# Three reorderings around an attention loop, and a loop body of two groups instead of one

## What is computed

```python
h = relu(layernorm(x))
q, k, v = h @ Wq.T + bq, h @ Wk.T + bk, h @ Wv.T + bv
scores = where(adj > 0, q @ k.T / sqrt(128), -9e15)
x = x + elu(softmax(scores) @ v)

h = relu(layernorm(x))
g = h @ W
s1, s2 = g @ a[:128, 0], g @ a[128:, 0]
e = where(adj > 0, leaky_relu(s1[:, None] + s2[None, :], 0.01), -9e15)
x = x + g + softmax(e) @ h
```

## Time and profile before

| | us |
|---|---|
| median of 3 runs | 750.28 |
| lowest, highest | 747.99, 750.70 |
| the profiled execution | 749.78 |
| its span, first to last instruction | 748.0 |
| PE busy in it | 716.1 |
| DVE busy | 566.5 |
| ACT busy | 539.8 |
| GpSimd busy | 458.8 |

### The profile page before, as it was taken

The page is one execution under the profiler, slowest core; times in us unless marked ns, Lnnn a source line. Parts: engine busy times, 40 slices in busy tenths (PEclk is TensorE's granted clock), DMA queues, the critical chain, the costliest instruction groups (busy, mean ns, idle before and its releaser), DMA issues. The chain is left out here.

```text
span 748.0 us, 18367 instructions
## 1 busy us (share of the span) xinstructions
PE 716.1 (96%) x6269; PEld 604.4 (81%) x6269; DVE 566.5 (76%) x1201; ACT 539.8 (72%) x1083; POOL 458.8 (61%) x396
## 2 busy tenths in 40 slices
PE   7979999999999999999999999967999999999997
PEld 6657878888888888888888878855888888888886
DVE  6978778787877878788787877759977477577572
ACT  4745877878777687776877778868597797887910
POOL 6778699999999999999999998794000000000000
PEclk9999999999999999999999999987999999999999
DMA  7289999997898988989888873984333442443200
GB/s 239 81 267 258 234 286 235 261 266 232 283 258 245 261 238 281 252 251 261 241 278 245 263 144 81 184 80 85 72 88 75 86 96 64 95 90 68 40 11 13
DMA packets 192783, 132.51 MB, mean 177 GB/s; under 512 B 173536, under 2 KB 180192, under 8 KB 184544
## 3 DMA queue, kind: packets, MB, share of 16 engines
q1 hardware_dynamic: 192000, 131.63, 67.0%
q10 hardware_dynamic: 576, 0.26, 0.1%
q0 software_dynamic: 160, 0.00, 0.0%
HBM read 71.04 MB, written 18.89 MB: 120 GB/s over the span
## 5 line engine op out<-in xcount | busy, mean ns | idle before, releaser
L801 ACT ACTIVATE scores<-scores,neg_max 128x1024 f32<-128x1024 f32 x128 | 146.0, 1142 | 51.8 <-DVE neg_max L932 51.8
L945 DVE TENSOR_TENSOR low<-scores 128x1024 bf16<-128x1024 f32 x96 | 139.7, 1455 | 40.9 <-ACT scores L801 40.9
L1204 PE MATMUL spare<-v_parts,hiT 128*128 128x256 bf16 x768 | 160.5, 273 | 0.0
L363 POOL TENSOR_SCALAR mask_both<-mask_bytes 128x2048 bf16<-128x2048 uint8 x64 | 154.1, 2408 | 5.4 <-POOL mask_bytes L358 0.4
L926 DVE CUSTOM_DVE_ANT_0 scores<-ps_s,mask_both 128x1024 f32<-128x1024 f32 x128 | 155.9, 1218 | 0.4 <-POOL mask_both L363 0.4
L358 POOL TENSOR_SCALAR mask_bytes<-adj_both 128x2048 uint8<-128x2048 int32 x64 | 146.4, 2304 | 5.5 <-DMA adj_both<-in_adj 4.6
L1200 PE MATMUL spare<-v_parts,lowT 128*128 128x128 bf16 x768 | 143.8, 219 | 3.2 <-DMA lowT<-low 3.1
L815 ACT ACTIVATE hiT<-spare 128x512 bf16<-128x512 bf16 (+1 forms) x128 | 102.4, 800 | 36.0 <-PE spare L1174 33.5
L1658 PE MATMUL ps_x<-q_parts,over_k 128*128 128x258 bf16 x1024 | 119.6, 278 | 7.7 <-issue 5.2
L1658 PEld LDWEIGHTS ps_x<-q_parts,over_k 128*128 128x128 fp8e4 x1024 | 100.9, 99 | 25.0 <-issue 5.4
L1139 PE MATMUL ps_s<-k_hi,q_strip 128*128 128x512 f32 x256 | 112.2, 438 | 2.2 <-PEq L83 1.9
(11 more groups left out here) (180 smaller groups left out, 1301.9 us busy)
## 6 DMA issues: line engine op xcount, KB each, us to landing
adj_both<-in_adj SPq DMA_DIRECT2D x64, 1024.0 KB, 5.2
mask_bytes_dram<-mask_bytes SPq DMA_DIRECT2D x32, 512.0 KB, 2.9
x_sb<-in_x SPq DMA_DIRECT2D x8, 256.0 KB, 7.9
out<-res SPq DMA_DIRECT2D x32, 64.0 KB, 1.6
lowT<-low SPq DMA_TRANSPOSE x96, 4.8
mask_both<-s_row_dram SPq DMA_DIRECT2D x2, 768.0 KB, 7.7
over_k<-mask_bytes_dram SPq DMA_TRANSPOSE x16, 4.7
scores<-mask_bytes_dram SPq DMA_TRANSPOSE x16, 4.5
```

What stands on the lines that cost most here:

```text
L363: return nc.gpsimd.tensor_scalar(out, src, -NEG, NEG, ALU.mult, ALU.add)
L801: nc.scalar.activation(sc, sc, ACT.Exp, bias=neg_max[:, bn:bn + 1], accum_out=row_sum[:, bn, k:k + 1]).then_inc(exp_done, 1)
L945: nc.vector.tensor_tensor(low[k][:], p, high_half(p), ALU.subtract).then_inc(low_done, 1)
L1204: last = nc.tensor.matmul(ps_a[:], high, v_parts[:, t, :, :], start=first, stop=final)
```

## The change

Four edits.

1. In the first stage DVE copies the turned weights before it takes the moments of chunk 2, instead of behind them; ACT copies the first `hT` before the third root; PE's wait for the copied weights stands behind its second block of transposes.
2. In period 0 DVE makes both `pT_low` first, then adds masks and takes low parts in turn, with low part 2 last. SP turns low part 0 before it loads strip 3.
3. GpSimd no longer weighs. DVE does `weigh_words(c, 1)` for chunks 0 and 1 behind `weigh(6)`, and GpSimd splits them behind the split of chunk 6.
4. The hardware loop of the attention runs over pairs of groups: three iterations with eight periods each, instead of six with four.

```diff
@@ norm_and_project
             roots(0)
             roots(1)
+            hT_out(0)
             roots(2)
-            hT_out(0)
...
+            hook("vector_early", dve, steps)
             moments_of(2)
             inverse(2)
-            hook("vector_early", dve, steps)
...
                 if c + 1 < NC:
                     to_hT(c + 1)
+                if c == 0:
+                    hook("tensor_first", pe)
...
                     last.then_inc(turn_done, 1)
+
+                def turned_in(pe):
                     pe.wait_ge(turn_read, 3)
@@ all_periods
-                    with eng.Fori(1, NC - 1) as c:
+                    with eng.Fori(0, NC // 2 - 1) as h:
                         for b in range(4):
-                            period(c, b)
+                            period(2 * h + 1, b)
+                        for b in range(4):
+                            period(2 * h + 2, b)
@@ sync
                         if b == 2:
                             store(0, 1)
-                    turn_low(0, 0, 0)
+                            turn_low(0, 0, 0)
@@ gpsimd
-                    def weigh_low(c):
-
-                        pool.wait_ge(s_out, pieces_till(c))
-                        for t in range(4 * c, 4 * c + 4):
-                            last = nc.gpsimd.tensor_scalar(v1[1][:, t, 0:D], h_sb[:, t, :], 0.0, v1[1][:, t, D:D + 1],
-                                                           ALU.max, ALU.mult)
-                        last.then_inc(low_weighed, 1)
-                        pool.wait_ge(low_weighed, c + 1)
-                        split_words(pool, c, 1)
...
                         split_words(pool, c, 0)
-                        if c < LOW_EARLY:
-                            weigh_low(c)
+                        if c == NC - 2:
+                            for n in range(LOW_EARLY):
+                                pool.wait_ge(low_weighed, n + 1)
+                                split_words(pool, n, 1)
@@ vector
                             inverse_sum(s - 1, (b + 3) % 4)
-                        if ahead:
+                        if not has(c, b, -1):
+                            turned_low(s, 0)
+                            turned_low(s, 1)
+                            add_mask(s + 1, bn, 2)
+                            low_part(s, b, 1)
+                            add_mask(s + 1, bn, 3)
+                            find_max(s + 1, bn)
+                            low_part(s, b, 2)
+                        elif ahead:
                             turned_low(s, 0)
                             low_part(s, b, 1)
                             add_mask(s + 1, bn, 2)
...
                     weigh(6)
+                    for c in range(LOW_EARLY):
+                        weigh_words(c, 1).then_inc(low_weighed, 1)
                     add_hw(3)
```

More of the change, by code:

```diff
@@ L518, in build @@
                                       scalar_chunk=first_strips, vector_early=copy_turned, tensor=constants_in,
-                                      tensor_early=turn_weights, tensor_chunk=extras, vector_chunk=copy_extras),
+                                      tensor_early=turn_weights, tensor_first=turned_in, tensor_chunk=extras, vector_chunk=copy_extras),
                                  [(q_product, q_high, q_low), (k_product, k_high, k_low), (v_product, v_high, v_low)],
```

## The result

| | before | changed kernel |
|---|---|---|
| median, us | 750.49 (4 runs, 747.99 to 751.13) | **760.67** (4 runs, 757.30 to 762.04) |
| ratio, 95% interval | | **1.0132** [1.0099, 1.0166] |
| profiled execution, its span | 749.78, 748.0 | 759.56, 757.6 |

A forecast was written before the change was run, and what follows sets the result against it. TensorE, busy 716.1 of 748.0 us, was taken to bound the kernel, with ACT and DVE pacing the loop. 749.78 + 0 - 1.8 - 3.4 + 5.3 = 749.9, forecast as 750.4 since the median lay 0.5 higher; range 743.5 to 756.0.

The forecast's parts named there:

- Less those 1.5 us that PE is early: Attention loop: PE's transposes end 1.5 us before ACT copies them, so a 3.3 us stall costs 1.8 per branch.
- The refetch of 3.3 us: PE's two backward branches: the doubled body's first code block is gone, and PE stands 3.3 us until it is fetched.
- The clock I counted for one branch of two: Behind PE's stall the clock is halved for 3.4 us, costing 1.7 us of work, counted once.
- the circle's pacemaker: Attention loop: the 13.28 us strip runs over ACT and DVE, with ACT's copy `pT_high` at 214.88; PE is not quite pacemaker.
- DVE may miss its own; I add nothing: Backward branches: DVE's doubled body may miss its first block, but would stand at the same moment as PE; 0 us.
- Splits, -3.4: End of the block: GpSimd only splits, so the engines' meeting point moves from 504.9 to 501.5; bounds -2.0 and -3.9.
- 0.3 us remain, and 0.2 us for DVE products that now run beside splits: End of the block: two more DVE products of 1.20 us, less a 2.11 us wait for ACT, plus 0.2 us slowing.
- Period 0, -1.8: Period 0: PE's 3.13 us stall goes, `low` 2 lands at 63.3, period 1 starts 1.8 us sooner; bounds 0, -4.8.
- First stage, 0: First stage: copies sooner leave the first `q_lo` where it was; 0 us, bounds 1.1 less and 0.5 more.
- Rival 1: Attention loop: PE's store holds nine blocks, only the reorderings count: 745.1 us, between 742 and 748; chance 0.30.
- Rival 2: PE's two backward branches: the refetch is long, at 5.2 us with the clock halved both times 755.9 us; chance 0.18.
- Rival 4: PE's backward branches: prefetch holds only two blocks, so the change saves three of five fetches: 739.7 us; chance 0.02.

The follow-up runs named there:

- PE alone: Kernel before with the three reorderings, and two groups an iteration on PE only, the other engines one: 760.42 us, ratio 1.0118.
- the reorderings alone: Kernel before with edits 1 to 3 and the loop left at six iterations of one group: 747.40 us, ratio 0.9957.
- the loop alone: Kernel before with the two-group loop on all engines and no reorderings: 759.79 us, ratio 1.0140.
- the unmoved one: Kernel before with the three reorderings and two groups an iteration on DVE only, without the 40 padding instructions: 746.86 us, ratio 0.9965.

## Why the prediction was wrong

I forecast 750.4 and the kernel takes 760.7. The mechanism was right: more packets, two stalls eight strips apart with no releaser, a lower clock behind one of them. It was put on one engine, and its price was halved by a slack that was not there when it was needed. At the branches this makes 5.0 us of the miss of 10; 2.9 are the splits, and 1.7 the other waits in the loop, for which the sum had no term.

**"Less those 1.5 us that PE is early" is the step that failed most.** It took 3.0 us off for two branches. The row that speaks against it was in my own first paragraph: PE works 99.4 of 100 us. An engine with 0.6 us of idle time in 100 has nowhere to make up a stall every eight strips. The run with PE alone shows it: 4.35 us of stall and slow clock cost 4.17, 6.68 cost 6.84. What I had read was a lead that PE had gathered slowly. In the kernel before, its first transpose comes 4.91 us after the row maximum in strip 5, 4.46 in strip 8 and 3.94 in strip 12 (212.29 - 208.35), 0.14 us less with each strip. In the changed kernel waits for `lowT` took it away on the way there. The kernel before, then the changed one:

```profile
212.29 0.27 PE L1153 MATMUL spare<-ident,scores 128*128 128x128 f32 x1
```

```profile
141.35 0.23 PE L1208 MATMUL spare<-v_parts,lowT 128*128 128x128 bf16 x1 [1.01 <-DMA lowT<-low]
...
181.53 0.23 PE L1208 MATMUL spare<-v_parts,lowT 128*128 128x128 bf16 x1 [0.62 <-DMA lowT<-low]
```

Without its stall PE would have been at this transpose 214.62 - 2.34 - 207.35 = 4.93 us after the maximum in the changed kernel (4.73 at the second branch), and 5.06 and 5.48 with PE alone. So of the 1.5 us 0.5, 0.7, 0.4 and nothing were left. What a stall costs an engine that still has its whole lead, no run shows.

**The refetch of 3.3 us was well sized for PE**: 2.34 and 2.77 us in the changed kernel, 2.65 and 4.98 with PE alone, 3.2 on average. The clock I counted for one branch of two; it fell behind one in the changed kernel, behind both with PE alone.

**ACT was left out.** I asked about PE and DVE, not about ACT, though its body had grown to 274 instructions as DVE's to 307. It stands 3.44 us at the first branch, at the very place that I had named as the circle's pacemaker, and ends later than PE there (at the second branch PE's transposes are last); alone it stands 3.18 and 3.01 us and costs nearly as much as all. Without the slack, 2 x 3.3 and 1.7 for the clock once make 8.3 instead of 5.3. Measured were 10.3. The other 2.0 lie, by the trace, where ACT comes later than PE and where `low` is slower behind it (2.06 us); how they divide was not tried.

**"DVE may miss its own; I add nothing"** was right in price, and DVE did not even miss. Its body, by luck of its place, touches three blocks.

**Splits, -3.4: the steady start moved by 1.0 in the reorderings alone, 0.5 in the change**, counted from the last row maximum. GpSimd's side was as forecast: it stopped being last. What failed is "0.3 us remain, and 0.2 us for DVE products that now run beside splits". Three products took 4.43 us where I had one at 1.20 and two more at the same rate, 0.8 more. `hT_diag` took 1.06 instead of 0.29. The wait of 2.11 us for ACT was used up, and PE stood 2.50 us (reorderings alone) instead of the 0.45 of the kernel before:

```profile
495.29 0.37 PE L1300 MATMUL ps_s<-ident,top 128*2 128x128 f32 x1 [0.45 <-DVE hT_diag L1114]
```

Then its 24 products ran 3.63 to 4.40 us instead of 2.94, partly at the halved clock.

**Period 0, -1.8:** measured 1.5 alone, 2.1 in the reorderings (99.32 - 46.34 = 52.98 from the first maximum to that of strip 4, against 55.10) and 2.5 in the change. As forecast, the 3.13 us stall went and a transposed low part was late next. But it was low part 1, for which PE waits inside period 0, and not low part 2 at the start of period 1 (63.65). That the size came out near -1.8 is therefore in part luck:

```profile
52.84 0.69 DVE L936 TENSOR_TENSOR pT_low<-spare,pT_high 128x512 bf16<-128x512 f32 x1 [1.12 <-ACT pT_high L806]
53.72 0.69 DVE L936 TENSOR_TENSOR pT_low<-spare,pT_high 128x512 bf16<-128x512 f32 x1 [0.19 <-ACT pT_high L806]
...
57.89 0.16 DVE L930 TENSOR_REDUCE neg_max<-row_max 128x1 f32<-128x4 f32 x1
...
62.33 0.22 PE L1208 MATMUL spare<-v_parts,lowT 128*128 128x128 bf16 x1 [1.79 <-DMA lowT<-low]
```

**First stage, 0:** not refuted. The first row maximum of the reorderings alone is at 46.34, before at 46.41, in single traces that differ by up to 3.8 us there.

**The rivals.** Rival 1 is out: nine blocks do not stay. Its price for the reorderings, 745.1, was 2.3 too low against the 747.4 measured, mostly by the splits. Rival 2, a long refetch, has the right sign and place but the wrong reason: the fetch was not long in the changed kernel (2.34 and 2.77 us), two engines had it, and almost nothing hid it. It had 0.18. Rival 4, the two-block rule on PE, is out too: PE's body of five blocks stays, in the kernel before and in every run with PE's one-group loop.

## What to carry to other kernels

Before you lengthen a loop body, count for each engine how many instruction blocks it touches, by its place and not only its length, and compare with a body whose queue is silent in the trace. A backward branch that misses cost nearly the whole stall on the engine that was nearly always busy, and on the one that feeds it; where a body does not stay, writing the loop out cost nothing here. And read slack from the idle time of the busiest engine in the stretch. How early one of its results is, is a lead that can be spent once, and must be read at the place where the stall will be.

## What the runs showed that I had not expected

- At a backward branch that misses PE stood 2.3 to 5.0 us and ACT 3.0 to 3.5 us (3.49 with the loop alone), DVE only 0.7 to 1.2. DVE's last instruction before the branch is one of 1.21 us and ACT's one of 0.30, which may be the difference; it was not tried.
- The packets of q14 are 8 KB, those of q8 16 KB (0.85 MB / 52). On ACT and DVE a body that reaches over three of these blocks stays and one over four does not; on PE five stay and nine do not. Between five and nine nothing was tried.
- The Trainium skill, "Runtime: NRT & Kernel Launch", section on instruction fetch mechanics, gives the engines other than PE 32 KiB in blocks of 16 KiB, and calls the store two lines. The trace agrees that a branch to code that is not there waits for a fetch. It disagrees on the packets, which are 8 KB on the queue of those engines, and on two lines for PE, where five blocks of 16 KB stay.
- Some 300 instructions of 64 bytes are 19 KB, and the place of such a body mattered more than its length: 68 instructions of padding took ACT's from 758.2 to 748.8 us. Whether the 8 KB packets are kept singly or in pairs no run decides.
- The 68 extra instructions on ACT in front of its loop cost nothing that shows; with the 40 on DVE PE waited 2.13 us for DVE there and was then given the lower clock, and the run is slower than the unmoved one (753.2 against 746.9 us, ratios 1.0022 and 0.9965).
- A DVE product of 128x512 takes 0.69 us alone and 1.2 to 1.5 us beside GpSimd's splits, and `hT_diag` 0.29 us before and 1.06 in the change.
